# Cross-attention on one core: contexts two units at a time, and the output weight's low-rank sum made in earlier batches

## The reference, cut to what matters

```
q = x @ Wq + 2 * (x @ Aq @ Bq)          # x: 8 batches of 256 x 1024; A, B of rank 16
k = c @ Wk + 2 * (c @ Ak @ Bk)          # c: 8 x 256 x 1024; 8 key/value heads of 32
v = c @ Wv + 2 * (c @ Av @ Bv)
scores = q k^T / sqrt(32)               # 32 query heads, 4 of them to a key/value head
context = softmax(scores) v
out = x + context @ Wo + 2 * (context @ Ao @ Bo)
```

## Time and profile before

| what | value |
|---|---|
| median of 3 runs | 676.45 us |
| the profiled execution, its own time | 678.06 us |
| its span, first to last instruction | 676.3 us |
| mean granted TensorE clock | 0.947 |
| PE, DVE, ACT, POOL busy | 662.5, 512.7, 467.6, 375.9 us |
| DMA queues' share of 16 engines | 59.6% |
| data moved | 125.07 MB |

### The profile page before, as it was taken

One profiled execution on the slowest core, in us unless ns is written; L12 is line 12 of the kernel. 1 busy time (PEld: TensorE's weight loads), 2 busy tenths in 40 slices (PEclk: granted clock), 3 DMA queues, 4 the chain that ended last, 5 costly groups with the idle time before them and its releaser, 6 DMA issues.

```text
span 676.3 us, 13385 instructions
## 1 busy us (share of the span) xinstructions
PE 662.5 (98%) x4220; PEld 528.2 (78%) x4220; DVE 512.7 (76%) x1161; ACT 467.6 (69%) x1462; POOL 375.9 (56%) x325
## 2 busy tenths in 40 slices
PE   9999999999999999999999999999899999999998
PEld 6798777877877887887887788787676788888886
DVE  4768887787788778778777877878887898855542
ACT  5558888888888888888888888887678443222220
POOL 3548785843762584386358438535867005776632
PEclk9999999999999999999999999999899999999999
DMA  8956655675665567556656646667676335655331
GB/s 268 355 171 211 207 182 164 196 212 167 174 197 183 158 195 227 162 179 195 198 149 201 210 157 183 197 187 211 186 225 205 107 120 172 202 187 186 126 121 66
DMA packets 103829, 125.07 MB, mean 185 GB/s; under 512 B 9280, under 2 KB 85312, under 8 KB 103760
## 3 DMA queue, kind: packets, MB, share of 16 engines
q1 hardware_dynamic: 103760, 124.23, 59.6%
HBM read 86.18 MB, written 38.01 MB: 184 GB/s over the span
## 4 chain that ended last, share of the span: by engine, by line
PE 82%; DVE 8%; ACT 4%; DMA 3%; issue 2%; SPq 1%; DVEq 0%
PE banks L1484 20%; PE banks L1677 17%; PE banks L1482 10%; PE banks L1502 9%; PE banks L1532 8%; PE banks L1519 8%; PE banks L1543 6%; DVE neg_max L1142 2%; ACT banks L930 2%; PE banks L1463 2%; DVE turned_sb L1163 2%; DMA raw<-xt 1%; PE banks L1450 1%; DVE max_parts L1151 1%; DMA raw<-ct 1%
## 5 line engine op out<-in xcount | busy, mean ns | idle before, releaser
L930 ACT ACTIVATE banks<-banks,neg_max 128x256 f32<-128x256 f32 x512 | 229.9, 452 | 29.8 <-DVE neg_max L1142 24.6
L812 POOL TENSOR_TENSOR q_stack<-turned_sb,head_mask 8x512 fp32r<-8x512 f32 x128 | 136.0, 1062 | 172.8 <-DVE turned_sb L1163 167.1
L1142 DVE TENSOR_REDUCE neg_max<-banks 128x2 f32<-128x512 f32 x256 | 175.0, 686 | 41.9 <-PE banks L1502 38.9
L941 ACT ACTIVATE probs_t<-banks 128x512 f32<-128x512 f32 x256 | 155.0, 605 | 48.4 <-PE banks L1519 48.0
L1484 PE MATMUL banks<-x_both,w_hi 128*128 128x512 f32 x448 | 162.9, 396 | 0.1
L1482 PE MATMUL banks<-x_both,w_lo 128*128 128x256 f32 x448 | 118.6, 280 | 0.0
L1502 PE MATMUL banks<-k_stack,q_stack 96*128 96x256 f32 x512 | 109.8, 296 | 0.7 <-DMA q_stack<-q_parts 0.7
L1502 PEld LDWEIGHTS banks<-k_stack,q_stack 96*128 96x128 f32 x512 | 81.3, 190 | 35.4 <-issue 25.8
L930 ACT ACTIVATION_READ_ACCUMULATOR banks<-banks,neg_max 128x1 f32 x512 | 106.7, 208 | 0.0
L1519 PE MATMUL banks<-q_stack,k_stack 104*128 104x512 f32 x256 | 102.4, 400 | 0.0
L1482 PEld LDWEIGHTS banks<-x_both,w_lo 128*128 128x128 f32 x448 | 84.5, 189 | 9.2
(11 more groups left out here) (156 smaller groups left out, 1154.7 us busy)
## 6 DMA issues: line engine op xcount, KB each, us to landing
q_stack<-q_parts SPq DMA_DIRECT2D x192, 128.0 KB, 3.0
q_parts<-q_stage SPq DMA_DIRECT2D x64, 256.0 KB, 3.5
raw<-ct SPq DMA_DIRECT2D x32, 256.0 KB, 3.5
raw<-xt SPq DMA_DIRECT2D x32, 256.0 KB, 3.8
scales<-r_rows SPq DMA_DIRECT2D x64, 128.0 KB
context<-ctx_stage SPq DMA_DIRECT2D x64, 128.0 KB, 3.7
stage<-xn SPq DMA_DIRECT2D x16, 512.0 KB, 5.4
w_hi<-context SPq DMA_DIRECT2D x14, 512.0 KB, 7.0
```

Of the source, the lines that this page charges most:

```text
L812: nc.gpsimd.tensor_tensor(q_stack[rows, u % RING, heads], turned_sb[rows, u % 2].unsqueeze(1).broadcast_to([M_ROWS, 2, S]), head_mask[rows ...
L930: last = nc.scalar.activation(score_bank(s)[:, S * h:S * (h + 1)], score_bank(s)[:, S * h:S * (h + 1)], ACT.Exp, bias=neg_max[:, u % 2, i: ...
L941: nc.scalar.activation(probs_t[:, u % 2, t, 2 * hp:2 * hp + 2, :].rearrange("p a b -> p (a b)"), st_bank[j % 2], ACT.Exp, scale=-1.0).then ...
L1142: nc.vector.tensor_reduce(out=neg_max[:, u % 2, 2 * c:2 * c + 2], in_=score_bank(s).rearrange("p (h t) -> p h t", h=2), axis=AXIS, op=ALU. ...
```

## The change

**Contexts in pairs.** Units 0 to 61 (of 64) are done two at a time. `context_pair` runs in the first slot of each odd unit and does the units three and two back: again eight matmuls, each with 32 stationary and now 512 moving columns (two heads of one unit), into a whole bank. `normalize_pair` does both units in one instruction, `store_pair` stores both. The exponentials of the transposed scores get a third buffer, in `w_sum`. The last two units are done singly as before. Rows of the context come out in another order, which the host puts into Wo and Ao.

**Rows of scaling factors.** `put_rows` writes each of the four rows four times, and `spread` reads them into 64 partitions of 512 elements, in place of 128 partitions of 256; it moves in SP's order, for an even unit behind the next unit's `put_rows`.

**Wo folded in four middle batches.** In batches 1 to 4 one tile is folded in slots 9, 17, 25 and 33: SP brings it into one of four buffers in `stage` (`fetch_raw`), PE makes the low-rank product in the context's bank (`wo_fold`), DVE adds (`wo_total`), SP stores the sum in DRAM (`keep_sum`). In the last batch SP loads the sums (`load_sum`); DVE copies the high part of the first eight, ACT of the others, POOL makes the low parts (`wo_low`). No fold matmul is left there. `load_sum` and the loads of x rows wait for `wo_lo`, that is for POOL, where `load_w` waited for DVE.

```diff
+WO_TILES = 2 * KT
+FOLD_AT, FOLD_PACE = 9, 8
+FOLD_BATCHES = 4
+COPIES = 4
+PAIRED = NB * NG - 2
...
+        p_room = [probs_t[:, 0], probs_t[:, 1],
+                  w_sum[:].rearrange("p a b -> p (a b)").rearrange("p (t h n) -> p t h n", t=2, h=GH)]
...
-        ctx_bank = banks[:, 4, 0:S]
+        ctx_bank = banks[:, 4, :]
...
+        def p_buf(n):
+
+            if n >= PAIRED:
+                return p_room[n % 2]
+            return p_room[(n + 1) % 3]
+
+        def contexts_before(n):
+
+            return n - 1 if n % 2 or n > PAIRED else n - 2
...
+        def fold_of(b, s):
+
+            k, off = divmod(s - FOLD_AT, FOLD_PACE)
+            if 1 <= b <= FOLD_BATCHES and s >= FOLD_AT and off == 0:
+                return 4 * (b - 1) + k
+            return None
...
+            def fetch_raw(n):
+
+                if 0 <= n < WO_TILES:
+                    need(sp, wo_kept, DMA * (n - 3))
+                    kt, half = n % KT, n // KT
+                    sp.dma_start(w_raw_o[n % 4], wo[kt, :, 512 * half:512 * (half + 1)]).then_inc(wo_raw_in[n % 2], DMA)
+
+            def keep_sum(n):
+
+                if 0 <= n < WO_TILES:
+                    wait(wo_summed, n + 1)
+                    sp.dma_start(wo_dram[n], w_raw_o[n % 4]).then_inc(wo_kept, DMA)
+
+            def load_sum(n):
+
+                wait(wo_kept, DMA * (n + 1))
+                if n % KT >= 4:
+                    wait(wo_lo, n - 3)
+                sp.dma_start(w_raw_o[wo_home(n)], wo_dram[n]).then_inc(wo_landed(n)[0], DMA)
...
                 def put_rows(g):
 
                     wait(turned_out, unit0 + (g + 2))
-                    sp.dma_start(r_dram[g % 2], turned_sb[KM:KM + GH, (g + 1) % 2]).then_inc(r_stored[g % 2], DMA)
+                    rows = turned_sb[KM:KM + GH, (g + 1) % 2]
+                    if unit0 + g < PAIRED:
+                        sp.dma_start(r_dram[g % 4].rearrange("(j r h) n -> h j r n", j=2, h=2),
+                                     rows.unsqueeze(1).broadcast_to([GH, COPIES, S])).then_inc(r_stored[g % 2], DMA)
+                    else:
+                        sp.dma_start(r_dram[g % 4, 0:GH], rows).then_inc(r_stored[g % 2], DMA)
...
+                    if unit0 + g < PAIRED:
+                        need(sp, ctx_done, unit0 + (g - g % 2))
+                        rows = P // 2 * (g % 2)
+                        sp.dma_start(scales[rows:rows + P // 2].rearrange("p a n -> p (a n)"),
+                                     r_dram[g % 4].rearrange("(j h) n -> j (h n)", h=2).unsqueeze(1).broadcast_to([2 * COPIES, HD // COPIES, 2 * S])
+                                     ).then_inc(r_spread[g % 2], DMA)
+                        return
...
                 late_loads(4, 5)
-                store_ctx(-1)
                 send(4)
-                spread(0)
                 stack_q(4, fills + 3, st0 + 4)
                 put_rows(1)
+                spread(0)
+                store_pair(-2)
                 late_loads(6, 7)
                 send(5)
                 spread(1)
-                store_ctx(0)
                 stack_q(5, fills + 3, st0 + 8)
                 put_rows(2)
                 first_loads(0, 1)
-                spread(2)
                 send(6)
+                wait(wo_lo, 6)
                 load_rows(0, 0)
...
+            def wo_low(n):
+                if n < KT:
+                    pool.wait_ge(wo_hi_dve, n + 1)
+                else:
+                    pool.wait_ge(wo_hi_act, n - KT + 1)
+                nc.gpsimd.tensor_tensor(wo_split(n, 1), w_raw_o[wo_home(n)], wo_split(n, 0),
+                                        ALU.subtract).then_inc(wo_lo, 1)
...
+            def wo_total(n):
+
+                dve.wait_ge(wo_folded, n + 1)
+                dve.wait_ge(wo_raw_in[n % 2], DMA * (n // 2 + 1))
                 nc.vector.scalar_tensor_tensor(
-                    out=w_piece(f, 0), in0=fold_bank(f), scalar=LORA_SCALE, in1=w_raw_of(f),
-                    op0=ALU.mult, op1=ALU.add).then_inc(w_hi_done, 1)
+                    out=w_raw_o[n % 4], in0=ctx_bank, scalar=LORA_SCALE, in1=w_raw_o[n % 4],
+                    op0=ALU.mult, op1=ALU.add).then_inc(wo_summed, 1)
+
+            def wo_high(n):
+
+                dve.wait_ge(proj_mm, (NB - 1) * PER + PRO)
+                dve.wait_ge(*wo_landed(n))
+                nc.vector.tensor_copy(wo_split(n, 0), w_raw_o[wo_home(n)]).then_inc(wo_hi_dve, 1)
...
+            def normalize_pair(b, u):
+                for i in range(2):
+                    dve.wait_ge(r_spread[i], b * (4 * DMA) + DMA * (u // 2 + 2))
+                    dve.wait_ge(ctx_stored[i], b * (4 * DMA) + DMA * (u // 2 + 1))
+                dve.wait_ge(ctx_mm, b * NG + (u + 2))
+                nc.vector.tensor_tensor(ctx_stage[:].rearrange("p a n -> p (a n)"), ctx_bank,
+                                        scales[:].rearrange("p a n -> p (a n)"), ALU.mult).then_inc(ctx_done, 2)
...
+            def wo_fold(b, s, n):
+
+                if n == 0:
+                    lora_o_ready(pe)
+                pe.wait_ge(ctx_done, b * NG + s // 4 - 2)
+                kt, half = n % KT, n // KT
+                nc.tensor.matmul(ctx_bank, lora_o[0][:, P * kt:P * (kt + 1)], lora_o[1][:, 512 * half:512 * (half + 1)],
+                                 start=True, stop=True).then_inc(wo_folded, 1)
...
+            def context_pair(b, u):
+
+                need(pe, ctx_done, b * NG + u)
+                need(pe, wo_summed, min(WO_TILES, 4 * (b - 1) + u // 2 + 1))
+                pe.wait_ge(st_exp, b * SLOTS + (4 * u + 8))
+                if u == 0:
+                    pe.wait_ge(v_moved, b + 1)
+                for t in range(2):
+                    for k in range(4):
+                        g, j = u + k // 2, k % 2
+                        last = nc.tensor.matmul(
+                            ctx_bank[HD * k:HD * (k + 1), :].rearrange("p (h n) -> p h n", h=2),
+                            v_sb[:, t, HD * (g % NG):HD * (g % NG + 1)],
+                            p_buf(b * NG + g)[:, t, j::2, :], start=(t == 0), stop=(t == 1),
+                            tile_position=(0, HD * k))
+                last.then_inc(ctx_mm, 2)
...
             def slot(b, s, first, last):
                 u, c = divmod(s, 4)
-                if last:
-                    for f in fold_chunks(s):
-                        if f == FOLD_O:
-                            lora_o_ready(pe)
-                        if f - FOLD_O in (0, 2, 4, 6, 8):
-                            pe.wait_ge(proj_out, b * PER + (PRO + (f - FOLD_O) // 2))
-                        fold_mms(f)
+                tile = fold_of(b, s)
+                if tile is not None:
+                    wo_fold(b, s, tile)
```

233 lines of the change are left out of this document (132 added, 101 removed).

## The result

The changed kernel takes **680.18 us** (median of 17 runs, 677.81 to 684.74) against 676.23 (17 runs, 675.62 to 677.22): ratio 1.0064 [1.0048, 1.0081]. It is slower by 0.6%, where 661.7 and faster was forecast. Its runs also scatter more, over 7 us against 1.6. The profiled execution took 677.81 us, the fastest of them; so the profile shows the losses at their smallest. That of the kernel before took 678.06, 1.8 us above its median, so the two profiles are nearly equally long where the medians are 4 us apart.

What follows compares the result with a forecast made beforehand. PE bounds the kernel, busy 662.5 of 676.3 us. Pairs -8.1, folds +3.7, last batch -8.4 and -2.0 sum to -14.8: span 661.5, 663.3 with the 1.76 around it, 661.7 us for the median; range 656.5 to 670.

Steps and rivals of the forecast that it cites:

- Pairs, -8.1: PE's contexts up to 464 us: a pair saves 0.30 us against two single contexts, 27 pairs save 8.1 us.
- Rivals B and C: A pair costs two contexts, 669.8 us, chance 0.06; four tiles not side by side at 512 columns, 676.7 us, 0.04.
- Folds, +3.7: Batches 1 to 4: 16 fold matmuls of 0.23 us each on PE add 3.7 us before 464 us.
- The step that failed: Folds in batches 1 to 4: PE waits of up to a microsecond per fold possible, taken as nothing.
- DMA "stays under 0.75": Middle batches: DMA, busy 0.60, gets 2 MB more a batch on 11 MB and stays under 0.75.
- The last batch, -10.4: Last batch: 8.4 us saved in slots 3 to 19, 2.0 us in slots 20 to 28.
- Rival A: Last batch: SP's loads wait for POOL's low parts and delay later queries; half clock returns; 668 to 669 us, chance 0.15.
- The failing step: Last batch, slots 3 to 19: 1.3 us of waits between four engines added to 26.7 us, giving 28.0.
- DVE's cast: Last batch, slots 3 to 19: a DVE copy of about 0.41 us per tile replaces two instructions of 0.69.
- Rival D: Scales for a pair's odd unit come too late and stop DVE, then PE; 685 us, chance 0.05.
- a sign of being wrong: PE waits over 5 us in all at a scores matmul for a DMA into q_stack.
- I gave slower 0.07: Whole kernel: chance 0.07 that the change makes it slower, beyond the 0.2% (1.35 us) told from no change.

Runs made afterwards that it cites:

- Short low parts: Changed kernel with DVE's low parts of x after batch 0 cut to 64 of 512 columns: 677.29 us, 1.0012.
- The light loads: Changed kernel with loads of the next context cut to 128 of 512 columns: 675.97 us, 0.9994; with DVE's low parts cut too, 670.34 us.
- the order tried first: Changed kernel with SP's copy of unit 7 moved ahead of load_context(3), send of k 1 and spread(3): 696.4 us, 1.0298.

## Why the prediction was wrong

- **Pairs, -8.1.** Right in mechanism, a little better in size: 0.41 for each pair by the intervals (0.37 by the block alone), 11.1 us in all, of which the time shows nothing. Rivals B and C are out.
- **Folds, +3.7.** Right: 0.24 each, no wait in front of them in this kernel. The run without them shows that their cost doesn't add to the time.
- **The step that failed** is "A cost of PE waits here is between nothing and a microsecond per fold [...]; I take nothing, since DVE has a slot or two in hand". It was taken from 49.4 of 58.5 us over the batch, and looked at the folds' waits only. A slot or two is 1.5 to 3 us; at slot 19 DVE had 1.0 us in hand, being busy 12.73 of 14.67 us in slots 12 to 20. The change took 1.1 us of it: 0.8 because the pair's block lets DVE's full stretch begin later while PE gets the time back from slot 16, and 0.3 by the wider multiplication. I had worked out the seven slots without a context for ACT, and not for DVE. Short low parts are worth 2.9 us alone, and 5.6 us where the loads are light already.
- **DMA "stays under 0.75".** True for the batch, 0.73, and no answer: the sum put nothing for a copy that lands later, and unit 7's took 4.8 us in place of 3.7. The light loads are worth 4 us alone, 10 with the first.
- **The last batch, -10.4.** Measured -2.0. Rival A came as described, with the half clock, but taking its wait away gave at most 1.7 of the missing 8.4, and nothing in the median. The failing step is "With four engines between 23 and 29 us of work [...] I add 1.3 us of waits". The order between them costs much more, though no run shows which engine sets it: between pairs PE is busy 12.4, 13.0 and 15.5 of 14.9, 15.6 and 17.4 us. DVE's cast was priced at 0.41 and took 0.74.
- **Rival D** didn't happen in the changed kernel (4.3 us of waits of DVE for the scales), but its mechanism came when the order was changed: in the order tried first SP gave to `q_stack` what it took from the scales.
- The prediction named a sign of being wrong, more than 5 us of waits for a DMA into `q_stack`. It came: 7.7 us in nine places.
- I gave slower 0.07. The rivals were each priced with the rest of the kernel standing still; none asked what PE meets next when it is 0.4 us a pair faster.

What stays open: what limits the last batch once rival A's waits are gone, and why kernels with the same program there differ by up to 2.8 us (64.3 to 67.1). The pairs, the new form of the spread and SP's new order came in one change, and no run keeps the pairs with the old order; so whether another order would have saved the 8 us isn't known.

## What to carry to other kernels

Before an engine that bounds is made faster, or its work is put into fewer and longer blocks, look at its partners slot by slot, and at the slots between the blocks above all: an average over the batch hides the one stretch where they have little slack. Ask what each queue's written order holds back there, for a wait that is taken away in such an order can be met again at the next place. To find out whether a gain is lost to waits, cut the work of the suspects one by one and together: here neither alone gave even half of what both gave.
